# S of the decay with queries as the stationary operand, in 64x32 parts of the array, and a transpose of masked S

## What is computed

```python
w = sigmoid(xn @ Wx @ Ww + bw); k = xn @ Wk; v = xn @ Wv; r = sigmoid(xn @ Wr)   # 4 heads of 64
def step(state, inp):
    kt, vt, wt, rt = inp
    state = (1.0 - wt)[..., None] * state + kt[..., None] * vt[..., None, :]
    return state, einsum('bhd,bhde->bhe', rt, state)
y = outs @ Wo
```

## Time and profile before

| | us |
|---|---|
| median of 3 runs (1003.62 to 1005.92) | 1005.36 |
| the profiled execution | 1006.33 |
| its span, first to last instruction | 1004.5 |
| TensorE busy | 965.0 |
| VectorE busy | 614.3 |
| ScalarE busy | 583.1 |
| GpSimd busy | 373.0 |
| mean granted clock of TensorE, share of full speed | 0.992 |

### The profile page before, as it was taken

One profiled execution on the slowest core, in us unless ns is written; L12 is line 12 of the kernel. 1 busy time (PEld: TensorE's weight loads), 2 busy tenths in 40 slices (PEclk: granted clock), 3 DMA queues, 4 the chain that ended last, 5 costly groups with the idle time before them and its releaser, 6 DMA issues.

```text
span 1004.5 us, 23095 instructions
## 1 busy us (share of the span) xinstructions
PE 965.0 (96%) x8840; PEld 812.0 (81%) x8840; DVE 614.3 (61%) x1285; ACT 583.1 (58%) x1439; POOL 373.0 (37%) x484
## 2 busy tenths in 40 slices
PE   4889999999999999999999999999999999998987
PEld 3667888888888888888888888888888888887875
DVE  3665758475575837557583755758375575837352
ACT  3555646566574656657465665746566574655331
POOL 1332525244352524435252443525244352524130
PEclk9899999999999999999999999999999999999999
DMA  8314231321322132232213213221321322122000
GB/s 292 97 48 125 59 114 47 97 77 58 107 73 91 47 96 78 58 107 76 86 49 97 77 58 107 69 91 51 96 78 59 106 75 76 49 86 58 12 1 22
DMA packets 58011, 79.00 MB, mean 79 GB/s; under 512 B 10288, under 2 KB 39856, under 8 KB 57904
## 3 DMA queue, kind: packets, MB, share of 16 engines
q1 hardware_dynamic: 56192, 76.38, 24.8%
q10 hardware_dynamic: 1712, 1.16, 0.4%
HBM read 73.05 MB, written 4.46 MB: 77 GB/s over the span
## 4 chain that ended last, share of the span: by engine, by line
PE 80%; DVE 8%; ACT 5%; issue 4%; POOL 2%; DMA 0%; DVEq 0%; POOLq 0%
PE gb L353 15%; PE scores L412 8%; PE acc L443 7%; PE gb L476 6%; PE scores L416 6%; PE acc L439 6%; PE ptp L426 6%; PE gb L537 5%; PE acc L444 5%; PE gb L586 3%; DVE xn L801 3%; PE gb L576 3%; PE gb L385 2%; ACT probs L651 2%; DVE probs L814 2%
## 5 line engine op out<-in xcount | busy, mean ns | idle before, releaser
L1040 POOL TENSOR_TENSOR t_l<-raw_t,t_h 128x516 fp32r<-128x516 f32 x128 | 167.3, 1307 | 206.9 <-PE scores L416 170.9
L651 ACT ACTIVATE probs<-scores,small 128x257 f32<-128x257 f32 x256 | 119.4, 472 | 149.8 <-DVE small L807 149.6
L807 DVE TENSOR_REDUCE small<-scores 128x2 f32<-128x514 f32 x128 | 88.3, 690 | 117.8 <-PE scores L416 117.3
L1049 POOL TENSOR_TENSOR ptm<-probs,head 128x32 f32<-128x32 f32 x128 | 35.2, 275 | 277.3 <-DVE probs L814 277.3
L814 DVE TENSOR_TENSOR probs<-probs,small 128x514 f32<-128x514 f32 x128 | 101.7, 794 | 4.4
L426 PE MATMUL ptp<-ident,probs 128*128 128x128 f32 x512 | 79.9, 279 | 13.3 <-DVE probs L814 11.9
L443 PE MATMUL acc<-pt,raw_n 128*128 128x256 f32 x256 | 89.6, 432 | 0.0
L412 PE MATMUL scores<-t_h,qk_h 128*128 128x258 f32 x256 | 84.1, 328 | 2.2 <-DVE qk_l L861 2.2
L662 ACT ACTIVATE pt<-ptp 128x512 f32<-128x512 f32 x128 | 77.3, 604 | 13.7 <-PE ptp L426 11.8
L439 PE MATMUL acc<-pt,raw_n 128*64 128x128 f32 x1024 | 83.2, 283 | 0.4 <-ACT pt L662 0.4
L1113 POOL TENSOR_TENSOR rstd<-ve,half 128x2 f32<-128x2 f32 x48 | 33.4, 696 | 124.4 <-ACT t_h L658 71.6
(11 more groups left out here) (168 smaller groups left out, 2758.2 us busy)
## 6 DMA issues: line engine op xcount, KB each, us to landing
raw_t<-in_ctx_t SPq DMA_DIRECT2D x128, 258.0 KB, 3.0
raw_n<-in_ctx_n SPq DMA_DIRECT2D x128, 192.0 KB, 2.4
xb<-in_x SPq DMA_DIRECT2D x16, 256.0 KB, 4.3
vsp<-tail_values SPq DMA_DIRECT2D x256, 2.0 KB
out<-ob SPq DMA_DIRECT2D x16, 256.0 KB, 2.8
xin<-in_x SPq DMA_DIRECT2D x15, 256.0 KB, 2.9
khat<-in_wq ACTq DMA_DIRECT2D x1, 512.0 KB, 4.5
wv<-in_wv SPq DMA_DIRECT2D x1, 512.0 KB, 6.4
```

The source lines that it names most:

```text
L651: go(probs[n % 2][:, r, 0:L], scores[:, r, 0:L], ACT.Exp, bias=nmax[:, r:r + 1], accum_out=rsum[:, r:r + 1]).then_inc(s["exp_ready"], 1)
L807: v_.tensor_reduce(nmax[:], scores[:, :, 0:L], AX.X, ALU.max, negate=True)\
L1040: p_.tensor_tensor(t_l[m % 2][:], raw_t[m % RING][:], t_h[m % 2][:].bitcast(F32), ALU.subtract)\
```

## The change

S is computed with queries stationary. For block i, the stationary operand is 64x32 of `rhat`, the moving one 64x128 of `khat`, and the result S[query, key] lands in partitions 32i to 32i + 31. Two heads and four blocks are thus eight parts of the array, 64 rows by 32 columns each. `rhat` is laid out block by block, and so are the rows of the mask. The masked S goes to a tile `s_q`; a new step `St` behind `pv` in step 0 transposes it with eight transposes of 128x128 into two tiles, St0 and St1, and ScalarE copies them into `s2`, which now lies in the first half of `hid` (free at that time). `o2_` waits for St1 and reads and writes with the queries' order permuted. The 1 that VectorE added to r is added by a second ScalarE pass, which waits for the Tanh, and VectorE's two operations become plain products.

```diff
-FILL2 = [[], ["Y3", "Y1", "XT"], ["Y2", "XT2", "q0", "q2"], ["z", "q1", "q3", "XT3"], ["k"], ["r"], ["Pf", "v"],
+FILL2 = [["St"], ["Y3", "Y1", "XT"], ["Y2", "XT2", "q0", "q2"], ["z", "q1", "q3", "XT3"], ["k"], ["r"], ["Pf", "v"],
...
-ENDING = {(NG, 0): [("Sq", OLD), ("WV", NEXT), ("Qf", OLDER)], (NG, 1): [("O2", OLD), ("Y3", OLDER), ("Y1", NEXT)],
+ENDING = {(NG, 0): [("Sq", OLD), ("WV", NEXT), ("Qf", OLDER)], (NG, 1): [("St", OLD), ("O2", OLD), ("Y3", OLDER), ("Y1", NEXT)],
...
-          (NG + 1, 0): [("Sq", NEXT), ("Y3", OLD), ("O2", NEXT)], (NG + 1, 2): [("Y2", NEXT)],
+          (NG + 1, 0): [("Sq", NEXT), ("Y3", OLD), ("St", NEXT), ("O2", NEXT)], (NG + 1, 2): [("Y2", NEXT)],
...
-        s2 = sb("s2", [P, 8, P])
+        s_q = sb("s_q", [P, 8, P])
+        s2 = hid[:, 0:4].rearrange("p c (a k) -> p (c a) k", a=2)
...
-                        block = slice(i * BLK, (i + 1) * BLK)
+                        queries = i * 2 * T // NB + (2 * c + t) * 32
                         for r0, out_ in ((0, even), (64, odd)):
-                            last = mm(out_[:, 0, t_].rearrange("p (b i) -> p b i", i=S)[:, :, block],
-                                      khat[r0:r0 + 64, keys:keys + P],
-                                      rhat[r0:r0 + 64, c * T + t * P:c * T + (t + 1) * P]
-                                      .rearrange("p (b i) -> p b i", i=S)[:, :, block], start=True, stop=True)
+                            last = mm(out_[32 * i:32 * i + 32, 0, t_],
+                                      rhat[r0:r0 + 64, queries:queries + 32],
+                                      khat[r0:r0 + 64, keys:keys + P], start=True, stop=True)
...
+            def turn_s(g):
+                for t in range(2):
+                    out_ = tile(f"St{t}", g)
+                    drained("S3", g)
+                    for h in range(4):
+                        last = nc.tensor.transpose(out_[:].rearrange("p a (c k) -> p (a c) k", k=P)[:, h],
+                                                   s_q[:, 4 * t + h], ident[:])
+                    done(f"St{t}", g, last)
+
             def o2_(g):
                 out_ = tile("O2", g)
-                drained("S3", g)
+                drained("St1", g)
...
-                    last = mm(out_[r0:r0 + 64, h // 2, t * P:(t + 1) * P], vt[:, t, h * 64:(h + 1) * 64], s2[:, j],
-                              start=True, stop=True)
+                    last = mm(out_[r0:r0 + 64, h // 2, t * P:(t + 1) * P]
+                              .rearrange("p (b i q) -> p i b q", i=NB, q=BLK), vt[:, t, h * 64:(h + 1) * 64],
+                              s2[:, j].rearrange("p (i b q) -> p i b q", i=NB, q=BLK), start=True, stop=True)
...
-                        act.wait_ge(s["tanh_ready"], g + 1)
+                        act.wait_ge(s["tanh_ready"], 2 * g + 1)
                         drain(n, g, go(at[:], at[:], ACT.Copy, scale=-0.5, bias=0.5))
                     elif n == "r":
-                        drain(n, g, go(rt_[:], t[:], ACT.Tanh, scale=0.5))
+                        go(rt_[:], t[:], ACT.Tanh, scale=0.5).then_inc(s["tanh_ready"], 1)
+                        act.wait_ge(s["tanh_ready"], 2 * g + 2)
+                        drain(n, g, go(rt_[:], rt_[:], ACT.Copy, bias=1.0))
...
+                    elif n[:2] == "St":
+                        to = s2[:, 4 * int(n[2]):4 * int(n[2]) + 4].rearrange("p h k -> p (h k)")
+                        drain(n, g, go(to, t[:].rearrange("p c k -> p (c k)"), ACT.Copy))
...
-                    drain(n, g, v_.copy_predicated(s2[:, 2 * c + e:2 * c + e + 5:4],
+                    drain(n, g, v_.copy_predicated(s_q[:, 2 * c + e:2 * c + e + 5:4],
...
-                        v_.scalar_tensor_tensor(rhat[:].rearrange(by_half, h=2, j=4)[:, :, h],
-                                                rt_[:].rearrange("p c t -> p (c t)").rearrange(by_half, h=2, j=4)
-                                                [:, :, h], 1.0, factor, ALU.add, ALU.mult)\
+                        v_.tensor_tensor(rhat[:].rearrange("p (i n h j) -> p n i h j", i=NB, h=2, j=4)[:, :, :, h],
+                                         rt_[:].rearrange("p c t -> p (c t)").rearrange(by_block, i=NB, h=2, j=4)
+                                         [:, :, :, h], factor, ALU.mult)\
...
-    t = np.arange(P)
-    key, query = t[:, None], t[None, :]
+    key = np.arange(P)[None, :]
+    query = np.arange(P).reshape(P // S, NB, BLK).transpose(1, 0, 2).reshape(P, 1)
```

More of the change, by code:

```diff
@@ L61 @@
 TILES.update({n: [n + "e", n + "o"] for n in ("Qa0", "Qa1", "Qb")})
-TILES.update({"Sp": ["S0", "S1"], "Sq": ["S2", "S3"]})
+TILES.update({"Sp": ["S0", "S1"], "Sq": ["S2", "S3"], "St": ["St0", "St1"]})
 SHIFT = {"XT": PREP, "TP": HERE}
@@ L66 @@
 SHIFT.update({n: POST for n in "WV Y1 XT2 z k r v Sp".split()})
-SHIFT.update({n: FFN for n in "Sq O2 Y2 XT3 Pf H0 H2".split()})
+SHIFT.update({n: FFN for n in "Sq St O2 Y2 XT3 Pf H0 H2".split()})
 SHIFT.update({n: END for n in ("Qf", "Y3")})
@@ L224, in build @@
         wr2_raw, wo2_raw = (x[:].rearrange("p c d -> p (c d)") for x in (at, xt2))
-        wo_raw = s2[:].rearrange("p t q -> p (t q)")
+        wo_raw = s_q[:].rearrange("p t q -> p (t q)")
         scores = ps("scores", [P, 2, 512])
@@ L603, in _ @@
                 steps[f"q{i}"] = lambda g, i=i: q(i, g)
+            steps["St"] = turn_s
             steps["Sp"], steps["Sq"] = lambda g: s_tiles(0, g), lambda g: s_tiles(1, g)
@@ L671, in step @@
             def step(name, g):
-                if name in ("Y1", "Y2", "Y3", "TP") or name[0] == "S":
+                if name in ("Y1", "Y2", "Y3", "TP", "Sp", "Sq"):
                     return
@@ L829, in decayed @@
                 dve.wait_ge(s["dec_ready"], DECAYS * g + k)
-            by_half = "p (m h j) -> p m h j"
             def step(n, g):
@@ L939, in step @@
                     decayed(g, 5)
-                    for h, factor in enumerate((inv[:].rearrange(by_half, h=2, j=4)[:, :, 0], pr[:])):
-                        v_.scalar_tensor_tensor(rhat[:].rearrange(by_half, h=2, j=4)[:, :, h],
-                                                rt_[:].rearrange("p c t -> p (c t)").rearrange(by_half, h=2, j=4)
-                                                [:, :, h], 1.0, factor, ALU.add, ALU.mult)\
+                    by_block = "p (n i h j) -> p n i h j"
+                    factors = (inv[:].rearrange(by_block, i=NB, h=2, j=4)[:, :, :, 0],
+                               pr[:].rearrange("p (n i) j -> p n i j", i=NB))
+                    for h, factor in enumerate(factors):
+                        v_.tensor_tensor(rhat[:].rearrange("p (i n h j) -> p n i h j", i=NB, h=2, j=4)[:, :, :, h],
+                                         rt_[:].rearrange("p c t -> p (c t)").rearrange(by_block, i=NB, h=2, j=4)
+                                         [:, :, :, h], factor, ALU.mult)\
                             .then_inc(s["rhat_ready"], 1)
@@ L982, in constants @@
                 v_.memset(vsp[:], 0.0).then_inc(s["zeros_ready"], 1)
-                v_.memset(s2[:], 0.0)
+                v_.memset(s_q[:], 0.0)
                 v_.memset(khat[:], 0.0)
```

## The result

| | before | changed |
|---|---|---|
| median, us (range) | 1005.64 (1003.62 to 1007.32) | 1033.22 (1032.74 to 1033.5) |
| span of the profiled execution | 1004.5 | 1030.9 |
| TensorE busy | 965.0 | 959.1 |
| ScalarE busy | 583.1 | 607.1 |
| mean granted clock | 0.992 | 0.975 |

The changed kernel is slower: the ratio is 1.027 (1.026 to 1.029). The forecast was 1031, in a range of 1012 to 1041. From span to span +26.0 was forecast, and it is +26.4.

A forecast was written before the change was run, and what follows sets the result against it. Two chains of nearly equal length, 11.3 us, TensorE's matmuls and ScalarE's queue, were taken to bound WV at 13 boundaries. Terms 12.3 + 4.5 - 1.9 - 2.5 + 13.6 = +26.0 gave 1031, range 1012 to 1041.

The forecast's parts named there:

- What bounds the kernel: Where step 7 passes into step 0: WV waits for S2's masked copy, behind ScalarE's exponentials; it is some 0.34 us late.
- the gate isn't S2's copy: Rival: WV's idle is only a cost of changing array parts, so all S savings reach the end: 990; chance 0.12.
- S: Steps Sp and Sq on TensorE: 32 instructions take 0.46 us instead of 1.71; with array-part changes Sp -1.05, Sq -1.15.
- not side by side: Rival: S's array parts don't run concurrently; 1024 with pairs as today, 1078 one at a time; chance 0.12, most near 1024.
- S at the 13 boundaries, worth 0: Step 7 to step 0 passages with table loads: TensorE's idle ahead of WV grows from 0.17 to about 2.3; nothing gained.
- The transposes: Eight of 128x128 behind pv in step 0, nothing hidden: 0.88 us each iteration, 14 iterations, +12.3.
- r's second pass: New ScalarE copy in step 5 delays pt_out and pv of step 6: +0.3 us each, 15 times, +4.5.
- The clock: Behind the new 2.3 us pauses ahead of WV, 8 of 13 bring a fall to half speed, 1.7 us each: +13.6.
- The boundary before the 13: Earlier step 7 to step 0 passage without Gelu or table load: Sq counts 1.15, Sp some 0.7, together -1.9.
- The ending: Last Sp and Sq, about -2.2, and the ending before it, -0.3: together -2.5, bounds -3.5 and 0.

The follow-up runs named there:

- early_mask_new: The changed kernel with VectorE's masks of S2 and S3 moved ahead of the normalization of the probabilities: 982.11 us, ratio 0.976 to the kernel before.
- st_twice: The changed kernel with those masks moved early and its eight transposes of masked S done twice: 996.61 us.
- r_behind_pt: The changed kernel with those masks moved early and r's second ScalarE pass moved from step 5 to step 6, behind pt_out: 981.5 us, ratio 0.975.
- after: The changed kernel itself, without any follow-up edit: 1033.22 us, ratio 1.027 to the kernel before.
- fill_1: The changed kernel with one filler matmul of TensorE in the pause ahead of WV, between the requests for WV's two banks: 1015.45 us.
- fill_2: The changed kernel with two filler matmuls of TensorE in the pause ahead of WV, between the requests for WV's two banks: 1013.26 us.
- before: The kernel before the change, without any edit: 1005.64 us.
- early_mask_old: The kernel before the change, with only VectorE's masks of S2 and S3 moved ahead of the normalization: 1002.21 us, ratio 0.996.
- r_alone: The kernel before with only r's part of the change: Tanh, wait, second ScalarE pass adding 1, plain products on VectorE: 1006.87 us, ratio 1.000.
- r_on_dve: The changed kernel with masks moved early and r's 1 added by VectorE in place instead of a second ScalarE pass: 997.78 us, ratio 0.992.

## Why the prediction was right, point by point

*What bounds the kernel.* Right. WV waits for S2's copy, which hangs on the exponentials. The changed trace fits it and `early_mask_new` shows it. The rival "the gate isn't S2's copy" fell with the same run. Its 990 was near what an open gate gives, 982, but the gate was the copy.

*S.* I took 0.46 and a tenth for each of two changes of array parts at Sp. The chain gives 0.60 with both of its ends, so 1.11 saved a step, where I had 1.05 and 1.15. Eight parts of 64x32 run side by side: the loads of all 32 instructions lie in 0.40 us (TensorE's weight loads at Sp):

```profile
538.51 0.40 PEld L540 LDWEIGHTS gb<-khat,rhat 64*32 64x32 f32 x32
```

That is 0.0125 us a load. The rule of the Trainium skill that the prediction weighed (TensorE: Matmul & The Clock Gate, "Wait — 56ns, not 53.3ns?") would have wanted twice that and a step of 0.80. The trace does not agree for matmuls on different parts of the array. The rival "not side by side" fell.

*S at the 13 boundaries, worth 0.* Right: 2.32 of idle time where 2.3 was forecast, all 13 times.

*The transposes.* Right: at the boundary of 429.08 pv of step 0 is 7.58 us later than before (425.48, now 433.06) and the next `turn_probs` 8.45 (426.98, now 435.43), so 0.87, the same as in `st_twice`. Nothing of them is hidden. The boundary as a whole, from step 7's `turn_probs` on, grew by only 0.82: the 0.05 less lie ahead of WV.

*r's second pass.* This term was mis-sized: 4.5 forecast, 1.4 for it and all the rest of the period in the changed trace, 0.8 at most alone. The step that failed is "+0.3 each". The delay is real (pv starts 0.40 behind the start of score's last group, 532.43 to 532.83, where it was 0.22), so 0.18 and not 0.3. The copies came as forecast: `pt_out` starts 0.54 behind the second pass, where I had 0.56. What I had too high is the hand-over: I took 0.14 from the end of `pt_out` to pv, and it is 0.05 (532.78 to 532.83):

```profile
531.03 0.60 ACT L725 ACTIVATE rt<-gb 128x512 f32<-128x512 f32 x1 [0.95 <-PE gb L356]
531.66 0.63 ACT L727 ACTIVATE rt<-rt 128x512 f32<-128x512 f32 x1
532.20 0.58 ACT L675 ACTIVATE pt<-ptp 128x512 f32<-128x512 f32 x1
```

And I stopped at the first waiter. I asked what waits for the late copy, found pv, and added the delay to the end, without asking what TensorE waits for next. That was `turn_probs`, for the probabilities, which took back about a third of it (0.12 is left there in the changed kernel); by `r_behind_pt` 0.08 an iteration stays at the end of the period.

*The clock.* 13.6 forecast; the falls at the boundaries cost 17.8: 11 and not 8, each 1.62 and not 1.7. The size of one was right, read from a single fall. The number was a guess between bounds, and the bounds held it.

*The boundary before the 13.* -1.9 with 0.88 for its transposes is -1.0, and it is -1.0. *The ending*: -2.5 forecast, -2.1 measured, but by luck. From the start of Qf to O2 the ending is 1.88 shorter: S saves 2.44, the transposes and ScalarE's copies take 1.83 in series, and the other 1.27 is the fall of the clock at 978.2 that only the kernel before has. I had counted on about as much from Y3 and filler starting earlier, and the clock there isn't in my rows. Without that fall the term is near -0.8.

*What the sum didn't hold.* The falls outside the boundaries. Start-up came 1.7 earlier. Of that, 1.1 is that the kernel before had a fall behind 1.93 us of idle time and the changed one had none behind the same pause. One more fall came in iteration 15, behind a pause of 1.86 ahead of 938.49, and cost 1.3. So the closeness of 26.0 and 26.4 is partly luck: r was 3 too high, the falls at the boundaries 4 too low, start-up and the extra fall nearly cancel, and the ending's term is right only with a fall that it didn't have.

## What to carry to other kernels

Taking work off the busiest engine gains nothing at a place where another engine's chain arrives at the same time. Follow the wait that comes next back to its start and see whether the work that you remove is on it: here a move of two masks ahead of a normalization, one line, turned +27 us into -24. An addition that looks hidden has to be followed past its first waiter, and so has a small operation that it pushes aside. And look at the length of a pause as well as at its sum: one filler matmul in each saved 18 us without starting WV any earlier. The clock has to be read in the kernel before as well: a fall that goes away with a change looks like a gain of its matmuls.

## What the runs showed of the hardware

- Pauses of TensorE and its clock, over the 12 traces: behind 2.32 us the clock fell 11 times of 13 (`after`). Behind 1.65 (`fill_1`) and 1.23 (`fill_2`) it never fell (26 pauses). In between it goes either way. The pause of 1.90 to 1.94 ahead of 59 to 60 us stands in each trace, and in four a fall followed (`before`, `fill_1`, `st_twice`, `r_behind_pt`). The one of 1.86 to 1.87 in iteration 15 was followed by one in five (`after`, the three with the masks early and no other edit, `r_behind_pt`), and that of 1.81 to 1.82 in the ending in one (`st_twice`). What decides between pauses of the same length was not tested. Apart from one of 10.2 us in start-up, a fall within the run lasts 3.4 us at half clock; it cost 1.62 at the boundaries and 1.1 to 1.4 elsewhere.
- The clock also fell while TensorE was busy by the profile: in the ending, 3.7 to 4.0 us behind the start of the 64 instructions of the old S, in all three kernels that have it (`before` 978.2, `early_mask_old` 973.2, `r_alone` 977.0). Behind the 64 of the new S, 1.26 us long, it fell in none of the other nine. That S is the cause was not tested.
- 32 instructions of 64x32 stationary and 128 moving columns, on eight parts of the array, start within 0.40 us, 0.0125 apart on average (`after`, 538.51).
- A VectorE operation of 128x2 took 1.21 us instead of 0.17 when it started 0.1 us into a GpSimd operation on 128x516, and 0.57 when it started 0.75 into it (`r_on_dve`).
- One and the same wait for a bank is given as "issue" in the changed kernel and as VectorE's copy in `fill_1`.
